# A two-layer gated attention kernel: the ternary layer's units run one slot earlier beside the first attention layer

## The reference, cut to what matters

```
x = x + tanh(g) * attention0(layernorm(x), ctx)          # 16 heads, 77 keys
x = x + tanh(g) * ternary(layernorm(x))                  # the layer that the change moves
x = x + tanh(g) * attention1(layernorm(x), ctx, bias)    # with a distance bias
x = x + tanh(g) * expert(layernorm(x))                   # ReLU layer and a layernorm

def ternary(x):          # quant: round(x * 127 / rowmax|x|), weights rounded to -1, 0, 1
    h = gelu(quant(x) @ w1)       # 256 -> 1024
    return quant(h) @ w2          # 1024 -> 256
```

## Time and profile before

| | us |
|---|---|
| median of 3 runs | 404.98 (404.76 to 409.9) |
| the profiled execution, its own time | 406.22 |
| its span, first to last instruction | 404.5 |
| granted TensorE clock over the span | 0.937 |
| attention layer 0, up to the first ternary slot of its own | about 0 to 173 |
| ternary slots 4 to 8 | about 173 to 204.7 |
| attention layer 1 and expert layer | 204.7 to 404.5 |

### The profile page before, as it was taken

The page is one execution under the profiler, slowest core; times in us unless marked ns, Lnnn a source line. Parts: engine busy times, 40 slices in busy tenths (PEclk is TensorE's granted clock), DMA queues, the critical chain, the costliest instruction groups (busy, mean ns, idle before and its releaser), DMA issues.

```text
span 404.5 us, 8923 instructions
## 1 busy us (share of the span) xinstructions
PE 329.9 (82%) x3222; PEld 271.4 (67%) x3222; DVE 282.7 (70%) x676; ACT 283.5 (70%) x516; POOL 230.9 (57%) x413
## 2 busy tenths in 40 slices
PE   2856878878866776878787899899877899999993
PEld 2646767667754453467566688788666799888882
DVE  6895568776777647989955557777856548666665
ACT  4366897799886777989934798866679755555550
POOL 4675644676577222457784755566775167444444
PEclk9996869998998868869999999999999999999998
DMA  8996431011100000320082222211100000000001
GB/s 242 278 179 170 92 86 41 10 39 43 42 6 17 2 0 2 52 25 2 2 257 53 50 53 53 52 35 27 45 2 2 2 0 29 28 28 27 28 28 52
DMA packets 23187, 22.02 MB, mean 54 GB/s; under 512 B 4711, under 2 KB 22504, under 8 KB 23067
## 3 DMA queue, kind: packets, MB, share of 16 engines
q1 hardware_dynamic: 23144, 21.45, 21.5%
HBM read 10.34 MB, written 2.10 MB: 31 GB/s over the span
## 4 chain that ended last, share of the span: by engine, by line
PE 46%; DVE 19%; ACT 17%; issue 10%; POOL 4%; DMA 3%; SPq 1%; ACTq 0%; POOLq 0%; DVEq 0%
PE psA L1723 10%; PE psA L1509 5%; PE psD L1707 5%; PE psBE L1707 4%; PE psD L1418 3%; ACT pp_hi L731 3%; DVE mx L1129 3%; PE psBE L1444 2%; DVE ham L1175 2%; DVE st L885 2%; ACT p L722 2%; PE psA L1493 2%; PE psA L1333 2%; DMA qb<-mT 2%; PE psA L1676 2%
## 5 line engine op out<-in xcount | busy, mean ns | idle before, releaser
L508 POOL TENSOR_TENSOR pp_lo<-p,pp_hi 124x512 f16<-124x512 f32 x80 | 92.7, 1178 | 46.6 <-ACT pp_hi L731 46.6
L404 POOL TENSOR_TENSOR lns<-lns,mhalf 128x2 f32<-128x2 f32 x39 | 31.0, 794 | 86.0 <-DVE lns L890 85.6
L1129 DVE TENSOR_REDUCE mx<-psBE 128x6 f32<-128x462 f32 (+1 forms) x96 | 54.5, 582 | 33.3 <-PE psBE L1444 32.9
L722 ACT ACTIVATE p<-psD 124x512 f32<-124x512 f32 x80 | 47.7, 597 | 27.8 <-PE psD L1418 27.1
L1418 PE MATMUL psD<-qb,ktb 98*124 98x256 f16 (+1 forms) x256 | 49.6, 291 | 12.1 <-DMA qb<-mT 10.3
L731 ACT ACTIVATE pp_hi<-p 124x512 f16<-124x512 f32 x80 | 50.4, 630 | 0.0
L1418 PEld LDWEIGHTS psD<-qb,ktb 98*124 98x124 f16 (+1 forms) x256 | 33.0, 145 | 16.9 <-DMA qb<-mT 13.2
L1444 PE MATMUL psBE<-kt_hi,q_hi 128*128 128x154 f16 (+2 forms) x160 | 34.0, 282 | 5.2 <-ACT mT L713 4.0
L1215 DVE TENSOR_TENSOR pp_lo<-space,pp_hi 128x512 f16<-128x512 f32 x32 | 25.7, 822 | 16.2 <-ACT space L834 15.5
L1723 PE MATMUL psA<-ew_hi,pp_hi 128*128 128x256 f16 x128 | 34.9, 273 | 0.0
L1723 PE MATMUL psA<-ew_hi,pp_lo 128*128 128x256 f16 x128 | 34.9, 273 | 0.0
(11 more groups left out here) (210 smaller groups left out, 1007.3 us busy)
## 6 DMA issues: line engine op xcount, KB each, us to landing
qb<-q_hi SPq DMA_DIRECT2D x32, 128.0 KB
xs<-in_x SPq DMA_DIRECT2D x8, 256.0 KB, 6.0
tw_raw<-in_tw SPq DMA_DIRECT2D x2, 1024.0 KB, 10.2
qb<-q_lo SPq DMA_DIRECT2D x16, 128.0 KB
space<-in_ew SPq DMA_DIRECT2D x2, 1024.0 KB, 6.5
out<-space SPq DMA_DIRECT2D x7, 256.0 KB, 2.1
ktb<-km SPq DMA_DIRECT2D x6, 248.0 KB, 7.9
qb<-bT_lo SPq DMA_DIRECT2D x8, 104.0 KB
```

The costliest lines, as they stand in the source:

```text
L508: nc.gpsimd.tensor_tensor(pl[:, u % 2, 2 * r:2 * r + 2, :], p32[:, n % 4, :, :], ph[:, u % 2, 2 * r:2 * r + 2, :], ALU.subtract).then_inc( ...
L722: a_(p32[:, n % 4, :, :], psD[n % 2][0:KR, :].rearrange("p (t r) -> p t r", t=2), ACT.Exp, scale=1.0 / SSC).then_inc(a["exp"], 1)
L1129: v.tensor_reduce(pairs[:, MP[k][0]:MP[k][1]:MP[k][2], :], psBE[:, n % 2, 0:hn * KEYS].rearrange("p (q e k) -> p q e k", e=2, k=KEYS), AX. ...
```

## The change

Unit 0's first tile is multiplied and gets its Gelu in slot 8, the second tile in slot 9, both through the two PSUM banks that the maxima used (psBE). Every later ternary unit up to 4 is one slot earlier, so the separate ternary slots are 5 to 8 instead of 4 to 8. The rounding (L809) of units 0 to 3 moves into the next attention slot, ahead of the next Gelu. On DVE the Gelu's maxima move to step 2 of slots 9 to 12 (behind the division of the attention, ahead of quantising); unit 4's maxima stand after slot 12. The statistics of attention unit 7 move from slot 11 to the end of slot 10. `tables_vo` moves to ternary slots 5 to 8, `keys_masked` to ternary slot 5, and two of the four `keys_high` into the first slots of layer 1; `split_low` moves from slot 9 to slot 7, the pieces of `ternary_round(1, i)` to (8, 2), (8, 4), (9, 1), (10, 1). POOL computes its factors before it waits for the attention's last transposes.

```diff
         def hps(n):
-            return (psD2, psBE)[n % 2][:, :, :]...
+            return (psD2 if n > 0 and n % 2 == 0 else psBE)[:, :, :]...
...
# POOL, normalise()
                 g = factors(n, scale)
+                if u == 0:
+                    pool.wait_ge(A[0]["pxT"], NU)
...
# ACT
+                    if l == 0 and (s, r) == (NU + 1, 1):
+                        ternary_hidden(0, (1,))
+                    if l == 0 and (s, r) == (NU + 2, 1):
+                        ternary_transposed(0, (1,))
...
                     if l == 0 and r == 4 and s == NU:
                         tables_v(1)
+                        ternary_hidden(0, (0,))
                     if r == 4 and l == 0 and s > NU:
-                        ternary_hidden(s - NU - 1)
+                        ternary_rounded(s - NU - 1)
+                        ternary_hidden(s - NU)
...
                 if l == 0 and 0 <= s - 4 < NU:
                     rounded(s - 4)
-                if l == 0 and s > NU:
-                    ternary_transposed(s - NU - 2)
+                if l == 0 and s == NU + 1:
+                    ternary_transposed(0, (0,))
+                if l == 0 and s > NU + 1:
+                    ternary_transposed(s - NU - 1)
...
-            for s in range(4):
-                attn_slot(0, NU + 1 + s)
+            for s in range(1, 5):
+                attn_slot(0, NU + s)
                 ternary_second(s)
-            for s in range(4, NU + 1):
+            for s in range(5, NU + 1):
                 ternary_slot(s)
...
# DVE
-                if l == 0 and s == 9 and r == 1:
+                if l == 0 and s == 7 and r == 5:
                     split_low(1, wraw[1, "o"], whl[1, "o"])
-                if l == 0 and (s, r) in ((8, 4), (9, 4), (10, 1), (11, 1)):
-                    ternary_round(1, s - 8)
+                if l == 0 and (s, r) in ((8, 2), (8, 4), (9, 1), (10, 1)):
+                    ternary_round(1, {(8, 2): 0, (8, 4): 1, (9, 1): 2, (10, 1): 3}[s, r])
...
+                    if l == 0 and r == 2 and s > NU:
+                        ternary_first(s - NU - 1)
...
+                if l == 0 and s == NU + 2:
+                    residual_stats(l, s - 3, ln)
-                if l == 0 and s > NU:
-                    ternary_first(s - NU - 1)
...
-                if 4 <= s < 8:
-                    if s == 4:
+                if 5 <= s < 9:
+                    if s == 5:
                         dve.wait_ge(A[0]["ppv"], 2 * NU)
-                    tables_v(1, s - 3)
+                    tables_v(1, s - 4)
...
-            for s in range(4):
-                attn_slot(0, NU + 1 + s, NU)
+            for s in range(1, 5):
+                attn_slot(0, NU + s, NU)
+                if s == 4:
+                    ternary_first(4)
                 ternary_second(s)
+            split_keys(1)
+            tables_v(1, 0)
+            for s in range(5, NU + 1):
+                ternary_slot(s)
+                if s == 5:
                     keys_masked(1)
+                if s in (6, 7):
+                    keys_high(1, s - 6)
             queries_lo(1, 0)
             attn_slot(1, 0, 3 * NU)
             ternary_slot(NU + 1)
+            keys_high(1, 2)
             attn_slot(1, 1, 3 * NU)
             ternary_slot(NU + 2)
+            keys_high(1, 3)
...
# PE, tables_vo()
                 if l == 1:
                     pe.wait_ge(A[0]["xTh"], NU)
-                    ge(pe, F["xTh"], k)
+                    pe.wait_ge(F["xTh"], k + 1)
...
+                    if l == 0 and (s, r) in ((NU, 3), (NU + 1, 0)):
+                        ternary_hidden(0, (s - NU,))
                     if r == 3 and l == 0 and s > NU:
-                        ternary_hidden(s - NU - 1)
+                        ternary_hidden(s - NU)
+                    if l == 0 and (s, r) == (NU + 2, 1):
+                        ternary_transposed(0, (1,))
...
-                if l == 0 and s > NU:
-                    ternary_transposed(s - NU - 2)
+                if l == 0 and s == NU + 1:
+                    ternary_transposed(0, (0,))
+                if l == 0 and s > NU + 1:
+                    ternary_transposed(s - NU - 1)
                 values(l, s - 2, 0)
```

More of the change, by code:

```diff
@@ L197, in hps @@
         def hps(n):
-            return (psD2, psBE)[n % 2][:, :, :].rearrange("p b c -> p (b c)")
+            return (psD2 if n > 0 and n % 2 == 0 else psBE)[:, :, :].rearrange("p b c -> p (b c)")
         def hTps(j):
@@ L528, in _ @@
             for u in range(NU):
-                if u == 0:
-                    pool.wait_ge(A[0]["pxT"], NU)
                 ge(pool, F["pxT"], u - 1)
@@ L769, in attn_slot, with ternary_hidden @@
                     rounded(s - 4)
-                if l == 0 and s > NU:
-                    ternary_transposed(s - NU - 2)
+                if l == 0 and s == NU + 1:
+                    ternary_transposed(0, (0,))
+                if l == 0 and s > NU + 1:
+                    ternary_transposed(s - NU - 1)
                 if s < NU:
                     shifts(l, s)
-            def ternary_hidden(u):
+            def ternary_hidden(u, halves=(0, 1)):
                 f = F
-                if u == 0:
-                    act.wait_ge(s_bias, 2)
                 if u < NU:
-                    for j in (0, 1):
+                    for j in halves:
                         n = 2 * u + j
@@ L783, in ternary_hidden @@
                         act.wait_ge(A[0]["dq"], u + 1)
+                        if n == 0:
+                            act.wait_ge(s_bias, 2)
                         if u > 0:
@@ L787, in ternary_hidden, with ternary_rounded, ternary_transposed @@
                         a_(h32[:, j, :], hps(n), ACT.Gelu, scale=dq1[:, n:n + 1]).then_inc(f["gelu"], 1)
-            def ternary_transposed(u):
+            def ternary_rounded(u):
+                f = F
+                for j in (0, 1):
+                    n = 2 * u + j
+                    act.wait_ge(f["amax"], u + 1)
+                    ge(act, f["phT"], n - 3)
+                    a_(hq[u % 2][:, j, :], h32[:, j, :], ACT.Identity, scale=ham[:, 2, j:j + 1],
+                       bias=epsc[:, 4:5]).then_inc(f["q1"], 1)
+            def ternary_transposed(u, halves=(0, 1)):
                 f = F
                 if 0 <= u < NU:
-                    for j in (0, 1):
+                    for j in halves:
                         act.wait_ge(f["phT"], 2 * u + j + 1)
@@ L802, in ternary_second @@
                 f = F
[L803 to L810, removed]
+                if 4 <= s < NU:
+                    ternary_rounded(s)
                 u = s - 4
@@ L1133, in attn_slot @@
                         divide(l, s - 3)
-                    if r == (1 if s < NU else 0) and 0 <= s - 4 < NU:
+                    if r == (1 if s < NU else 0) and 0 <= s - 4 < (NU - 1, NU)[l]:
                         residual_stats(l, s - 4, ln)
+                    if l == 0 and r == 2 and s > NU:
+                        ternary_first(s - NU - 1)
                     if r == 1 and l == 1 and 0 <= s - 5 < NU:
@@ L1274, in _ @@
                     tables_v(0, 0)
-            for s in range(4):
-                attn_slot(0, NU + 1 + s, NU)
+            for s in range(1, 5):
+                attn_slot(0, NU + s, NU)
+                if s == 4:
+                    ternary_first(4)
                 ternary_second(s)
-                if s == 2:
-                    split_keys(1)
-                    keys_masked(1)
[L1281 to L1287, removed]
+            split_keys(1)
[3 more added lines that the diff above has]
+                if s == 5:
+                    keys_masked(1)
+                if s in (6, 7):
+                    keys_high(1, s - 6)
             queries_lo(1, 0)
@@ L1627, in before, with ternary_hidden @@
                         pe.wait_ge(F["gelu"], 2 * NU)
-            def ternary_hidden(u):
+            def ternary_hidden(u, halves=(0, 1)):
                 f = F
[L1631 to L1634, removed]
                 if u < NU:
-                    for j in (0, 1):
+                    for j in halves:
                         n = 2 * u + j
                         pe.wait_ge(A[0]["xTh"], u + 1)
-                        ge(pe, f["gelu"], n - 1)
+                        if n == 0:
+                            pe.wait_ge(s_tw, 4)
+                            pe.wait_ge(A[0]["mTc"], NU)
+                        if n == 2:
+                            pe.wait_ge(A[0]["exp"], 5 * NU)
+                        ge(pe, f["gelu"], n - 1 if n > 1 else n)
                         for c in (0, 1):
@@ L1644, in ternary_hidden, with ternary_transposed @@
                         i.then_inc(f["pm1"], 1)
-            def ternary_transposed(u):
+            def ternary_transposed(u, halves=(0, 1)):
                 f = F
-                if u == 0:
-                    pe.wait_ge(s_v32, 2)
-                    pe.wait_ge(A[0]["norm"], NU)
                 if 0 <= u < NU:
```

(14 more changed lines are left out.)

## The result

The changed kernel takes 409.23 us in the median (405.96 to 411.9, 20 runs), the kernel before 405.88 (20 runs on the same chips). The ratio is 1.0097, 95% interval 1.0075 to 1.0119: the change costs 3.9 us (3.0 to 4.8), where +1.7 was forecast. All ratios here leave out executions over 1.5% slower than the fastest of the same kernel, five of 20 for the kernel before, none for the changed one and three of eight for e4; over all 20 the medians differ by 3.35 us and the means by 3.0. The median of 409.23 lies inside the stated range of 402.3 to 409.4, and 0.9 us of its distance to the stated 406.7 come from the kernel before, whose median was 404.98 in 3 runs and is 405.88 in 20; but the change itself costs over twice what was forecast. The profiled execution has a span of 408.5 us, 4.0 above the old one.

The account below looks back on a forecast made before the run. ACT, busy 67.98 of 80 us from 124 to 204 us, was taken as the limit, with DVE's list order using up the lead. -0.4 + 1.3 + 0.8 = +1.7 on 404.98 gave 406.7 us, range 402.3 to 409.4.

Parts of the forecast that it names:

- The walk through slots 9 to 12: Slots 9 to 12: roundings of units 0 to 4 expected at about 137, 147, 159, 170 and 176.5 us.
- gain 0.4 us: Ternary slots up to unit 7's rounding: it comes at 199.1 us against 199.45 before, a gain of 0.4 us.
- The ring: Slots 11 and 12: DVE's maxima wait behind the preceding unit's second matmul, residual and statistics; 11.3 us against 9.2 of ACT work.
- The table loads: ACT, slots 8 and 9: three Exp/Gelu table loads in place of one, +2.6 us, no drain added.
- Ternary slot 8, "+1.3 us": PE, ternary slot 8: tables_vo waits for copy L814 ahead of unit 7's transposes, delaying layer 1's first queries by 1.3 us.
- Layer 1, "+0.8": DVE, layer 1's slot 1: a keys_high ahead of the first maximum adds 0.8 us; the one in slot 2 adds 0.
- three signs of being wrong: Unit 3's rounding before 166 us, PE's clock near 1.0 in 160 to 180, or layer 1's queries before 203.
- the one of a cold PE: Rival: from slot 9 on PE never gets full clock, costing +4.4 us, total 411; chance 0.12.
- in ternary slots 5 to 7 the same wait hides: Ternary slots 5 to 7: the wait of tables_vo for ACT's copy hides under the Gelu.

Follow-up runs that it names:

- e4: Changed kernel with DVE doing residual and statistics of ternary units 0 and 1 behind the maxima of units 2 and 3; ratio 0.9955 to the kernel before.
- e1: Changed kernel with idle PE time filled by unread matmuls in ternary slot 8 and in layer 1's slot 1; ratio 1.0034 to the kernel before.
- e3: Changed kernel with tables_vo of ternary slot 8 behind unit 7's transposes on PE's list; ratio 1.0040 to the kernel before.
- e7: Changed kernel with the edits of e2, e3 and e4 together; ratio 0.9867 to the kernel before.
- e8: Changed kernel with the edits of e7 and e6 together; ratio 0.9892 to the kernel before.
- e10: Changed kernel with the edits of e7 and e9 together; ratio 0.9902 to the kernel before.
- e5: Kernel before with only the last two keys_high moved behind ternary slots 9 and 10, into layer 1's first slots; ratio 0.9995 to the kernel before.
- e6: Changed kernel with unit 0's two Gelus together in slot 9 behind the last exponent, one table load instead of three; ratio 1.0115 to the kernel before.
- e11: The kernel of e5 once more, unchanged, to look at the clock; slot 1 of layer 1 took 18.80 us.
- e12: The changed kernel once more, nothing altered; slot 1 of layer 1 took 18.80 us, unit 7's rounding came at 83.75 us.
- e16: The changed kernel again, nothing altered; slot 1 of layer 1 took 18.80 us, unit 7's rounding came at 84.83 us.
- e9: Changed kernel with the edit of e6, but unit 0's two tiles in different PSUM banks; ratio 1.0104 to the kernel before.
- e15: The changed kernel again, nothing altered; slot 1 of layer 1 took 20.47 us, unit 7's rounding came at 83.91 us.
- e2: Changed kernel with its two late keys_high put on DVE into ternary slot 8 instead of layer 1's first slots; ratio 1.0075 to the kernel before.

## Why the forecast was half of the cost

- **The walk through slots 9 to 12** was right: in the first trace no rounding of units 0 to 4 was off by more than 2.1 us, and those of units 2 to 4 by 0.4. Its end, "gain 0.4 us", is near the mean lead of 0.7: counted from the mark, unit 7's rounding comes at 85.20, 85.24, 82.81, 82.58 and 85.21 us in the five traces with the old list (mean 84.2), at 83.08, 82.99, 83.09, 83.09, 83.75, 83.91 and 84.83 in seven with the new list up to there (mean 83.5). The lead of the first pair of traces, 2.1 us, is chance. That the walk ends so near the mean is in part luck too: from unit 4's rounding to unit 7's it counted 22.6 us, and the seven traces took 21.3 to 21.9; and it measured its gain against one trace of the kernel before, which happened to show the later of the two values.
- **The ring** was right in slot 12, in place and size: 11.3 us expected, 11.3 to 12.2 measured from unit 2's rounding to unit 3's; e4 cut it and unit 7 came 3.4 us earlier. In slot 11 it bound less than forecast: ACT waited 0.58 us in the first trace and up to 1.88 in the others.
- **The table loads** were right: three of 1.28 us, and nothing beside them. The second Gelu load starts at 133.96, 0.02 us after the instruction ahead ends, the other two 0.02 and 0.03. The drain that the Trainium skill (ScalarE: Activation LUTs, section "What ACT_TABLE_LOAD costs") adds to each switch shows at none of the three; the measurement decides.
- **Ternary slot 8, "+1.3 us", is the step that failed.** It measures +3.05 in the mean of eight traces with this order of PE's list and no filler (10.21 to 10.24 against 7.16 to 7.19). I counted the wait and 0.55 us of matmuls, with the work behind them at full clock ("0.9 (16 transposes, warm)"), in a slot where PE had just been given 1.35 us more to wait. With the clock held up (e1) it is +1.40. The term lacked the 1.65 us that the fallen clock costs. With the wait gone from that place the length is 7.68 to 7.70 in all four traces (e3, e7, e8, e10).
- **Layer 1, "+0.8", is short in the same way**, but only in part of the executions: +0.70 with the clock up, +2.37 with it fallen. Of ten traces with the late `keys_high` and no filler, five show 18.8 us (e5, e6, e11, e12, e16) and five 20.5 (the first profile, e3, e4, e9, e15); mean +1.5. With these `keys_high` in DVE's idle time all four traces show 18.09 (e2, e7, e8, e10).
- With these means the sum is -0.7 + 3.05 + 1.5 = +3.9 us, inside the measured 3.0 to 4.8. That it meets the 3.9 to a tenth is chance: by their own scatter (an estimate from the values above) the mean lead is good to about 0.7 us and the mean of slot 1 to 0.3, and what lies ahead of the mark is left out.
- None of the three signs of being wrong appeared: unit 3's rounding starts at 170.36, the clock of 160 to 180 us is 0.74, the first query matmuls start at 206.41. None of them watched PE's clock in ternary slot 8 or behind it.
- Of the rivals, the one of a cold PE was put in the wrong place. It said slots 9 and 10; there the first trace has a mean clock of 0.95 (138 to 160 us) where the old one has 0.77 (e12 and e15 have 0.80 and 0.84), and it fell in the two places where the change makes PE wait longer. I had written "in ternary slots 5 to 7 the same wait hides", looked for the cost of each moved item in its own duration, and never asked what an added wait does to the work behind it, though the earlier trace rows show that link.
- Open: why 2.27 us of waiting costs the clock in half of the traces. The instructions are the same; the start of the stretch within the execution differs. No run here varied that by itself.

## What to carry to other kernels

Where an edit lengthens a wait of PE, price the matmuls behind it at both clock levels, not only the wait: here 1.65 us came on top of 1.4 and of 0.7. Where two lists are shifted against each other by a slot, follow one unit around all engines and ask whether anything it waits for stands behind something that waits for it; the order of two items on DVE was worth 3.4 us. Take several traces before you call a difference of 2 us in one stage a result, and measure it from a mark inside the trace.

## What the runs showed of the hardware

- Matmuls that nobody reads made the kernel faster: 15 of them, 3.3 us of PE time in idle places, took 3.3 us off the two stretches, with the granted clock at 1.00 instead of 0.70 to 0.88.
- The same wait of 2.26 to 2.27 us left PE's clock up in five traces and was followed by its fall in five; the length of slot 1 is then 18.8 or 20.5 us, with no value between.
- DVE ran slower beside POOL's large subtraction (124x512) and not beside its small operation (128x2): `split_low` took 1.08 us next to it in the changed kernel and 0.69 in its old place, where POOL ran the small one for part of the time. The prediction read its pair of 2.07 and 1.27 us as with and without busy POOL; in the trace POOL was busy in both, with the large one for half of the first and the small one for most of the second.
